# When GpSimd issues its scatters of rows and of weighted outputs in a sparse mixture of experts

## The chip, the cores and the metric

The kernel runs on one core of a Trainium2 chip. The time is device microseconds (us) of that core from a run of the whole program; lower is better. The core has five engines that run side by side and meet at semaphores: TensorE (PE, with its weight loads as PEld), VectorE (DVE), ScalarE (ACT), GpSimd (POOL) and SyncE (SP), which here only issues transfers.

## What is computed

Two layers, each a gated cross attention and a gated mixture of experts, over 8192 tokens of 128 channels. The change lies in the last mixture, which sends each token to the best two of eight experts:

```python
logits = jnp.einsum('bsd,de->bse', x, Wg)
top_vals, top_idx = jax.lax.top_k(logits, TOP_K)          # 2 of 8
probs = jax.nn.softmax(top_vals, axis=-1)
...
    u = jnp.einsum('bsd,dh->bsh', x, W1[e])
    v = jnp.einsum('bsd,dh->bsh', x, W2[e])
    h = u * jax.nn.sigmoid(u) * v
    y = jnp.einsum('bsh,hd->bsd', h, W3[e])
    out = out + y * weights[..., e][..., None]
```

It runs on the layer-normed x, and its result is added to x with a gate.

## The kernel before

**Groups and sends.** The tokens are worked on in 16 groups of 512 (four tiles of 128). The dense part (mixture of layer 0, attention of layer 1, routing for the last mixture) runs over the groups in a software pipeline. Once a group is routed, its rows are *sent*: POOL issues eight indirect transfers a group (two choices times four tiles, line 1208), each of 128 rows of 130 floats, into a table in HBM sorted by expert (`sorted_rows`). Groups 14 and 15 are the last ones and are sent while the sparse part already runs.

**The sparse mixture.** The sorted table is cut into 135 tiles of 128 rows, each of one expert (`DTILES` = 135). The loop over them is written out as *steps*, one function `sparse(t)` an engine. In step t, SP has loaded the rows of tile t (line 1168, seven buffers), PE transposes them (L1977), multiplies tile t-3 with the expert's two first matrices (L1965) and tile t-6 with its last one (L1982), ACT copies weights (L1728) and applies silu (L1734), and DVE keeps the transposed rows (`d_xT`, L1466, one per step and the first thing of a step), multiplies the hidden values (L1471), scales the output of tile t-6 by the token's share (L1484, into one of 32 buffers `shares`) and copies weights (L1490). PE ends a step by adding one to the semaphore `ends_mm`; DVE begins its step t by waiting for that. PE in turn may be a few steps ahead of DVE: its step t needs what DVE kept in step t-3.

**Contributions.** The scaled output of each tile is written to HBM by one indirect transfer of POOL, 128 rows of 128 floats (`keep_share`, line 1224, tile name `contributions`), at the place of each row's token. 135 of them are issued. At the end the contributions are loaded back by group and added to X. For groups 0 to 13 that begins at step 88.

**What sets the order on POOL.** POOL's instructions stand in the order of the code and run in it. During the sparse mixture each of its transfers waits for a step that is written by hand: `scatter_paced(n, steps)` issues the eight sends of group n, the i-th behind the end of step `steps[i]` on PE; `keep_share(t, step)` issues the contribution of tile t behind the end of `step` and behind DVE's share t. Both go through `after_step`, a wait on `ends_mm`. A share can leave at step t+7 at the earliest. In the kernel before, the sends of group 14 are tied to steps 6 to 10, six contributions to steps 11 to 14, the sends of group 15 to steps 15 to 20, and the other contributions follow ten steps behind the earliest step, a distance that shrinks by one every eight tiles and is gone at tile 86.

**Who waits for POOL.** DVE takes a share's buffer again 32 tiles later and waits for the contribution that left it (`kept`, line 1482; first in step 38). SP waits for the sends of groups 14 and 15 before it loads tile 56, and for contributions from step 89 on, before it loads them back.

Of the kernel before, what the change touches and what calls it, by code (L numbers as in the profile page):

```python
# [32 lines left out]
DTILES = 2 * G * GW // P + E1 - 1  # L33
# [32 lines left out]
def wait_alone(eng, semaphore, value):  # L66

    eng.wait_ge(semaphore, value)
    eng.nop(nofuse=True)
# [696 lines left out]
def within(n):  # L766
    return 0 <= n < G
# [215 lines left out]
def mixtures_and_attention(nc, sb, psum, sem, c, a, X, dispatch, out):  # L983
# [71 lines left out]
    HIDDEN, OUT = 3, 6  # L1055
# [62 lines left out]
    def blocks_kept(eng, blocks):  # L1118

        for i in range(8):  # L1120
            tiles = sum(min(4, DTILES - 4 * b) for b in range(i, blocks, 8))
            eng.wait_ge(kept[i], 16 * tiles)
# [9 lines left out]
    def group_sent(eng, n):  # L1132

        eng.wait_ge(dispatch.sent[n % 2], 16 * 2 * GT * (n // 2 + 1))

    with nc.Block() as block:
# [41 lines left out]
        @block.gpsimd  # L1178
        def _(pool):
            def spread_deviation(ln, n):  # L1180
                if within(n):
                    ln.deviation(pool, n)
                    ln.offset(pool, n)

            def deviation1(n):
                if within(n):
                    ln1.deviation(pool, n)

            def number_rows(n):

                if within(n):
                    if n >= 2:
                        group_sent(pool, n - 2)
                    for k in range(2):
                        last = pool.tensor_copy(send[n % 2][k][:, :, D], dispatch.places[:, k, bass.ts(n, GT)])
                    last.then_inc(numbered, 1)

            def scatter(n, which):
                if within(n):
                    if which[0] == 0:  # L1200
                        pool.wait_ge(numbered, n + 1)
                        pool.wait_ge(top1.op_done, top1.ops * (n + 1))
                        wait_alone(pool, place_step, PLACE_STEPS * (n + 1))
                    if which[0] == GT:
                        wait_alone(pool, second_row_ready, n + 1)
                    for i in which:
                        k, j = i // GT, i % GT
                        pool.indirect_dma_start(dispatch.rows, bass.IndirectOffsetOnAxis(ap=slots[n % 2][:, k, j:j + 1], axis=0),  # L1208
                                                send[n % 2][k][:, j, :], None).then_inc(dispatch.sent[n % 2], 16)

            def after_step(step):

                wait_alone(pool, ends_mm, min(step, DTILES + OUT - 1) + 1)

            def scatter_paced(n, steps):
                for i, step in enumerate(steps):
                    after_step(step)
                    scatter(n, (i,))

            def keep_share(t, step):  # L1220

                wait_alone(pool, share_ready, t + 1)
                after_step(step)
                pool.indirect_dma_start(dispatch.contributions, bass.IndirectOffsetOnAxis(ap=token[:, t % KEEP:t % KEEP + 1], axis=0),  # L1224
                                        shares[t % KEEP], None).then_inc(kept[t // 4 % 8], 16)

            pool.memset(w_padded[:].rearrange("p t n -> p (t n)"), 0.0)
            pool.memset(chosen[:].rearrange("p t e -> p (t e)"), 0.0).then_inc(set_up, 1)
            for i in STEPS:
                spread_deviation(ln2, i - 5)  # L1230
                scatter(i - 6, (0, 1))
                deviation1(i - 3)
                scatter(i - 6, (2, 3))
                spread_deviation(ln, i + 1)
                scatter(i - 6, (4,))
                number_rows(i - 5)
                scatter(i - 6, (5, 6, 7))
            spread_deviation(ln2, 14)
            number_rows(14)
            scatter_paced(13, (0, 0, 1, 1, 2, 2, 3, 3))  # L1240
            spread_deviation(ln2, 15)
            number_rows(15)
            scatter_paced(14, (6, 6, 7, 8, 8, 9, 10, 10))
            for t, step in enumerate((11, 12, 12, 13, 14, 14)):
                keep_share(t, step)
            scatter_paced(15, (15, 16, 16, 17, 18, 18, 19, 20))
            for t in range(6, DTILES):
                keep_share(t, t + OUT + 1 + max(0, 10 - (t - 6) // 8))
            blocks_kept(pool, BLOCKS)

        @block.vector
# [875 lines left out]
```

## Time and profile before

| | us |
|---|---|
| median of 3 runs | 858.91 (858.59 to 859.61) |
| the profiled execution | 859.59 |
| its span, first to last instruction | 857.8 |

The rows further down come from the profiled execution. Times in them are from the span's start. A timeline row has start, duration, engine, line, operation, what is written and read, how many instructions, and in brackets the idle time of the engine before it and what ended it ("issue": nothing that the profile shows; "remote": a semaphore whose giver the profile doesn't name). A row of a table of stretches has the stretch, its length, then busy time and number of instructions of an engine, then the granted clock of TensorE (1.00 is full speed, 2.4 GHz), the busy share of the transfer engines, and GB/s. Starts of PE's matmuls are recorded and their ends are modelled. Steps are found by counting the rows of L1466, one for each.

### The profile page before, as it was taken

How to read it: one execution, taken by the hardware profiler on the slowest of the kernel's cores; microseconds unless marked ns; L12 is line 12 of the kernel's file. 1: busy time of each engine (PE TensorE's matmuls, PEld its weight loads, DVE VectorE, ACT ScalarE, POOL GpSimd, SP SyncE). 2: the span in 40 equal slices, each digit the busy share in tenths (PEclk: the TensorE clock that was granted, in tenths of full speed). 3: DMA queues.
4: the chain of work that ended last, by engine and by line, in shares of the span. 5: the costliest groups of instructions: out<-in, count | busy, mean ns of one | idle time of the engine just before them, and what ended most of it. 6: DMA issues, size and time to landing. Idle time of an engine off the chain costs nothing. (4 is left out here: it accounts for less than half of the span.)

```text
span 857.8 us, 27845 instructions
## 1 busy us (share of the span) xinstructions
PE 752.8 (88%) x9217; PEld 588.2 (69%) x9217; DVE 675.5 (79%) x2969; ACT 552.7 (64%) x1195; POOL 462.9 (54%) x498
## 2 busy tenths in 40 slices
PE   4899999999998979989989988777689898999991
PEld 2567666666666646766766765567689788888991
DVE  3899999999998968887888887646567666578993
ACT  2778787788787656888888786535445444444550
POOL 3455445544565011366776776664556666565564
PEclk9999999999999979999999999977899999999996
DMA  9101100010000010011111111121233333266764
GB/s 255 57 25 34 34 21 21 21 43 21 21 21 3 2 41 1 21 35 43 51 48 43 51 45 38 47 68 47 54 73 94 89 81 81 76 180 201 228 186 128
DMA packets 59177, 56.41 MB, mean 66 GB/s; under 512 B 9976, under 2 KB 49177, under 8 KB 59081
## 3 DMA queue, kind: packets, MB, share of 16 engines
q1 hardware_dynamic: 41736, 33.16, 14.6%
q0 software_dynamic: 8416, 17.38, 6.1%
q10 hardware_dynamic: 8928, 4.70, 1.9%
q8 instruction: 47, 0.77, 0.4%
q14 instruction: 50, 0.40, 0.2%
HBM read 32.65 MB, written 22.56 MB: 64 GB/s over the span
## 5 line engine op out<-in xcount | busy, mean ns | idle before, releaser
L1224 POOL DMA_INDIRECT contributions<-v_heads,d_token x135 | 133.2, 986 | 87.3 <-PE bc_bank L1982 47.8
L1208 POOL DMA_INDIRECT sorted_rows<-r_send,r_slots x128 | 127.0, 992 | 47.0 <-issue 40.6
L1965 PE MATMUL bc_bank<-d_xT,d_w 128*128 128x128 f32 x608 | 88.1, 291 | 13.4 <-DVE v_heads L1484 6.6
L1466 DVE COPY d_xT<-bc_bank 128x128 f32<-128x128 f32 x135 | 38.4, 284 | 73.5 <-PE bc_bank L1982 48.1
L512 POOL TENSOR_SCALAR a_k_heads<-a_kT,first 128x512 f32<-128x512 f32 x60 | 93.4, 1569 | 3.7 <-ACT a_kT L567 3.7
L1965 PEld LDWEIGHTS bc_bank<-d_xT,d_w 128*128 128x128 f32 x608 | 79.3, 204 | 16.8 <-DVE d_xT L1466 15.3
L1728 ACT COPY d_w<-w 128x512 f32 x135 | 83.4, 618 | 1.8 <-issue 0.6
L429 DVE TENSOR_REDUCE a_neg_max<-a_scores 128x16 f32<-128x1024 f32 x64 | 78.0, 1219 | 7.0 <-PE a_scores L680 6.1
L705 PE MATMUL a_probsT_bank<-first,a_probs 128*128 128x128 f32 x512 | 80.2, 279 | 0.3
L426 DVE TENSOR_REDUCE a_denom<-a_probs 128x16 f32<-128x1024 f32 x64 | 78.4, 1224 | 1.7 <-issue 1.3
L598 ACT COPY a_probsT<-a_probsT_bank 128x512 f32<-128x512 f32 x128 | 74.7, 584 | 6.3 <-PE a_probsT_bank L705 6.3
L591 ACT ACTIVATE a_probs<-a_scores 128x1024 f32<-128x1024 f32 x64 | 65.6, 1025 | 19.2 <-PE a_scores L691 19.2
L1734 ACT ACTIVATE b_weighted<-bc_pair 128x256 f32<-128x256 f32 x59 | 22.8, 387 | 79.4 <-PE bc_bank L1965 48.7
L680 PE MATMUL a_scores<-a_k_heads,a_qT 32*64 32x256 f32 x1024 | 70.8, 391 | 2.5 <-ACT a_kT L567 2.3
L1965 PE MATMUL bc_pair<-d_xT,d_w 128*128 128x128 f32 x472 | 65.6, 283 | 6.0 <-DVE d_xT L1466 4.1
L74 POOL TENSOR_SCALAR a_rstd<-a_stats 128x4 f32<-128x4 f32 x16 | 3.7, 233 | 121.1 <-DVE a_stats L396 121.1
L705 PEld LDWEIGHTS a_probsT_bank<-first,a_probs 128*128 128x128 f32 x512 | 57.9, 142 | 15.2 <-issue 12.5
L1965 PEld LDWEIGHTS bc_pair<-d_xT,d_w 128*128 128x128 f32 x472 | 59.2, 197 | 8.4 <-DVE d_xT L1466 5.8
L1804 PE MATMUL bc_bank<-b_xnT,w 128*128 128x512 f32 x96 | 51.1, 645 | 13.0 <-ACT c_kT L1653 7.1
L1734 ACT ACTIVATE b_hidden<-bc_bank 128x256 f32<-128x256 f32 x68 | 26.4, 390 | 43.4 <-PE bc_pair L1965 20.8
L1982 PE MATMUL bc_bank<-w_in,b_hidden 128*128 128x128 f32 x272 | 44.2, 280 | 4.6 <-issue 3.1
L1855 PE MATMUL bc_bank<-w,b_weighted 128*128 128x128 f32 x384 | 46.8, 278 | 0.1
(236 smaller groups left out, 2022.7 us busy)
## 6 DMA issues: line engine op xcount, KB each, us to landing
d_rows<-sorted_rows SPq DMA_DIRECT2D x135, 65.0 KB
X<-in_x SPq DMA_DIRECT2D x16, 256.0 KB, 3.1
b_hidden<-contributions SPq DMA_DIRECT2D x8, 512.0 KB
b_weighted<-contributions SPq DMA_DIRECT2D x8, 512.0 KB
out_x<-X ACTq DMA_DIRECT2D x16, 256.0 KB
ctxT<-in_ctx_T SPq DMA_DIRECT2D x16, 192.0 KB, 3.0
c_ctxT<-in_ctx_T SPq DMA_DIRECT2D x16, 192.0 KB
contributions<-v_heads,d_token POOLq DMA_INDIRECT x135
```

The source lines that it names most:

```text
L426: dve.reduce_sum(denom[:], probs[u % 2][:].rearrange("p (h k) -> p h k", k=S), AX_X).then_inc(sum_done, 1)
L429: dve.tensor_reduce(neg_max[:], scores[u % 2][:].rearrange("p a (h k) -> p (a h) k", k=S), AX_X, ALU.max, negate=True).then_inc(max_done, 1)
L512: last = pool.tensor_scalar(keys_of_head(par, j), kT[:], c.head_of_group[:, j:j + 1], None, ALU.mult)
L591: act.activation(probs[(u + 1) % 2][:], scores[(u + 1) % 2][:].rearrange("p a n -> p (a n)"), ACT.Exp, scale=SCALE0).then_inc(exp_done, 1)
L598: act.copy(probsT[u % 2][:, half * HU // 2:(half + 1) * HU // 2, :].rearrange("p u q -> p (u q)"), probsT_bank[:]).then_inc(pT_ev, 1)
L680: last = pe.matmul(scores[u % 2][S * b:S * b + S, s, bass.ts(h, 4 * S)], qT[par][rows_in, h, tile, :], k_heads[par][rows_in, tile, h].rear ...
L705: last = pe.transpose(probsT_bank[:, bass.ts(k, P)], probs[u % 2][:, bass.ts(half * HU // 2 + k, P)], c.ident[:])
L1208: pool.indirect_dma_start(dispatch.rows, bass.IndirectOffsetOnAxis(ap=slots[n % 2][:, k, j:j + 1], axis=0), send[n % 2][k][:, j, :], None) ...
L1224: pool.indirect_dma_start(dispatch.contributions, bass.IndirectOffsetOnAxis(ap=token[:, t % KEEP:t % KEEP + 1], axis=0), shares[t % KEEP], ...
L1728: act.copy(w12[t % W12][:], c.w12[:, bass.ds(experts[t % 4], 1)].rearrange("d a i h -> d (a i h)")).then_inc(w12_ready, 1)
L1804: pe.matmul(h_bank[k][:], c.w1_0[:, 2 * k:2 * k + 2, :].rearrange("d e h -> d (e h)"), xnT[n % 2][:], start=True, stop=True).then_inc(h_mm ...
L1965: last = pe.matmul(uv(m)[:, bass.ts(i, P)], w12[m % W12][:, bass.ts(i, P)], xT[m % TURNED][:], start=True, stop=True)
```

## The change

Only the table of steps on POOL changes:

```diff
             scatter_paced(13, (0, 0, 1, 1, 2, 2, 3, 3))
             spread_deviation(ln2, 15)
             number_rows(15)
-            scatter_paced(14, (6, 6, 7, 8, 8, 9, 10, 10))
-            for t, step in enumerate((11, 12, 12, 13, 14, 14)):
-                keep_share(t, step)
-            scatter_paced(15, (15, 16, 16, 17, 18, 18, 19, 20))
-            for t in range(6, DTILES):
-                keep_share(t, t + OUT + 1 + max(0, 10 - (t - 6) // 8))
+            scatter_paced(14, (14, 14, 15, 15, 16, 16, 17, 17))
+            scatter_paced(15, (18, 18, 19, 19, 20, 20, 21, 21))
+            for t in range(DTILES):
+                keep_share(t, max(t + OUT + 1, 22 + 10 * t // 13))
             blocks_kept(pool, BLOCKS)
```

`OUT` is 6. All 16 sends now stand behind steps 14 to 21, two a step. The contributions come behind them: the first at step 22, then 13 in ten steps, until the rule t+7 takes over at tile 61. Number, size and content of the transfers are the same.

On POOL, from the last four sends of group 14 to the first contributions (names: `r_send` the rows of a group by choice, `v_heads` the memory in which the shares lie, `d_ends_mm` the end of a step on PE, `d_share` DVE's share), as one piece of the difference:

```order
 L1208 DMA sorted_rows<-r_send_1,r_slots 67456x130 [waits d_ends_mm,r_second_row]
 L1208 DMA sorted_rows<-r_send_1,r_slots 67456x130 [waits d_ends_mm] x3
-L1224 DMA contributions<-v_heads,d_token 18304x128 [waits d_share,d_ends_mm] x6
 L1208 DMA sorted_rows<-r_send_0,r_slots 67456x130 [waits d_ends_mm,r_place_step,r_numbered,r_op_done]
 L1208 DMA sorted_rows<-r_send_0,r_slots 67456x130 [waits d_ends_mm] x3
 L1208 DMA sorted_rows<-r_send_1,r_slots 67456x130 [waits d_ends_mm,r_second_row]
 L1208 DMA sorted_rows<-r_send_1,r_slots 67456x130 [waits d_ends_mm] x3
-L1224 DMA contributions<-v_heads,d_token 18304x128 [waits d_share,d_ends_mm] x129
+L1224 DMA contributions<-v_heads,d_token 18304x128 [waits d_share,d_ends_mm] x135
```

Six contributions moved from between the two groups of sends to behind both; the steps for which the rows wait are in the diff.

On DVE, step 38, the first that waits for a contribution to have left its buffer, before:

```order
L1466 COPY d_xT<-bc_bank 128x128 [waits d_ends_mm]
L1467 COPY d_ends<-d_rows 128x2
L1471 TENSOR_TENSOR b_weighted<-b_weighted,bc_pair 128x256 [waits d_silu_done]
L1483 CAST d_token<-d_ends 128x4 [waits d_row_read,d_kept0]
L1484 TENSOR_SCALAR v_heads<-bc_bank,d_ends 128x128
L1490 ISA
L1490 COPY w_in<-w 128x256
```

and now:

```order
L1464 COPY d_xT<-bc_bank 128x128 [waits d_ends_mm]
L1465 COPY d_ends<-d_rows 128x2
L1469 TENSOR_TENSOR b_weighted<-b_weighted,bc_pair 128x256 [waits d_silu_done]
L1481 CAST d_token<-d_ends 128x4 [waits d_row_read,d_kept0]
L1482 TENSOR_SCALAR v_heads<-bc_bank,d_ends 128x128
L1488 ISA
L1488 COPY w_in<-w 128x256
```

Nothing moved here but the line numbers; only when `d_kept0` comes can differ.

## Rows read from the trace of the kernel before

**Rows 1.** The page's first part: busy time, share, instructions.

```profile
PE 752.8 (88%) x9217; PEld 588.2 (69%) x9217; DVE 675.5 (79%) x2969; ACT 552.7 (64%) x1195; POOL 462.9 (54%) x498
```

**Rows 2.** Stretches of the sparse mixture, L1466 alone: its count is the steps.

```profile
602.00:624.00 22.00, 2.31 (x8) 0.77 0.23 62
624.00:640.40 16.40, 2.29 (x8) 1.00 0.27 65
640.40:652.80 12.40, 2.25 (x8) 1.00 0.37 93
652.80:727.10 74.30, 11.60 (x41) 0.97 0.33 84
727.10:768.10 41.00, 6.26 (x22) 0.97 0.43 121
768.10:837.20 69.10, 11.78 (x42) 1.00 0.71 204
```

**Rows 3.** The first two stretches, sends (L1208) alone.

```profile
602.00:624.00 22.00, 7.84 (x8) 0.77 0.23 62
624.00:640.40 16.40, 7.74 (x8) 1.00 0.27 65
```

**Rows 4.** The same two, contributions (L1224) alone.

```profile
602.00:624.00 22.00, 3.83 (x4) 0.77 0.23 62
624.00:640.40 16.40, 1.92 (x2) 1.00 0.27 65
```

**Rows 5.** The later stretches, columns PE, PEld, DVE, ACT, POOL; POOL issues contributions only.

```profile
640.40:652.80 12.40, 12.40 (x112) 12.14 (x112) 10.24 (x50) 6.36 (x15) 6.80 (x7) 1.00 0.37 93
652.80:727.10 74.30, 65.79 (x531) 62.43 (x530) 46.79 (x218) 35.28 (x86) 45.41 (x47) 0.97 0.33 84
727.10:768.10 41.00, 36.98 (x300) 35.11 (x298) 26.72 (x122) 17.07 (x42) 24.86 (x26) 0.97 0.43 121
768.10:837.20 69.10, 64.83 (x535) 61.30 (x535) 61.77 (x263) 35.43 (x83) 42.14 (x42) 1.00 0.71 204
```

**Rows 6.** Timeline of POOL in steps 9 to 11.

```profile
607.15 1.01 POOL L1208 DMA_INDIRECT sorted_rows<-r_send,r_slots  x1 [2.20 <-PE bc_bank L1982]
...
614.80 0.96 POOL L1208 DMA_INDIRECT sorted_rows<-r_send,r_slots  x1 [0.30 <-issue]
617.87 0.96 POOL L1224 DMA_INDIRECT contributions<-v_heads,d_token  x1 [2.11 <-remote]
```

**Rows 7.** Timeline of PE: ends of steps 11 and 12, begin of step 13.

```profile
610.67 0.61 PE L1982 MATMUL bc_bank<-w_in,b_hidden 128*128 128x128 f32 x4
...
613.01 0.61 PE L1982 MATMUL bc_bank<-w_in,b_weighted 128*128 128x128 f32 x4
618.19 2.04 PE L1965 MATMUL bc_bank<-d_xT,d_w 128*128 128x128 f32 x8 [4.56 <-DVE v_heads L1484]
```

**Rows 8.** Timeline of DVE: begins of steps 11, 12 and 14.

```profile
617.13 0.29 DVE L1466 COPY d_xT<-bc_bank 128x128 f32<-128x128 f32 x1 [5.08 <-remote]
...
619.83 0.28 DVE L1466 COPY d_xT<-bc_bank 128x128 f32<-128x128 f32 x1
...
624.06 0.29 DVE L1466 COPY d_xT<-bc_bank 128x128 f32<-128x128 f32 x1 [1.42 <-PE bc_bank L1982]
```

**Rows 9.** Timeline of POOL, steps 37 to 45: bursts of five and of four contributions.

```profile
661.61 0.96 POOL L1224 DMA_INDIRECT contributions<-v_heads,d_token  x1 [1.34 <-PE bc_bank L1982]
...
666.78 0.96 POOL L1224 DMA_INDIRECT contributions<-v_heads,d_token  x1 [0.30 <-issue]
669.49 0.96 POOL L1224 DMA_INDIRECT contributions<-v_heads,d_token  x1 [1.75 <-PE bc_bank L1982]
...
676.02 0.96 POOL L1224 DMA_INDIRECT contributions<-v_heads,d_token  x1 [1.66 <-PE bc_bank L1982]
```

**Rows 10.** Timeline of PE: end of step 38.

```profile
663.91 0.61 PE L1982 MATMUL bc_bank<-w_in,b_hidden 128*128 128x128 f32 x4
```

**Rows 11.** Timeline of DVE: begin of step 38.

```profile
668.76 0.29 DVE L1466 COPY d_xT<-bc_bank 128x128 f32<-128x128 f32 x1 [3.22 <-remote]
```

## The prediction

> **What bounds the kernel now.** I read the page's first part, then the sparse mixture by stretches of steps, then single bursts in the timelines. The page makes PE the busiest engine at 88% of the span, and POOL one of the emptiest at 54% [rows 1]. By that alone a change that only shifts POOL's transfers would seem free. The stretches say otherwise. In steps 22 to 29 the eight steps take 12.40 us, PE is busy for all 12.40 of them, and POOL issues only 7 transfers: 1.55 us a step. In steps 30 to 70, 41 steps take 74.30 us, 1.81 each, with 47 transfers, and PE is busy for only 65.79 of it [rows 2, 5]. Per step the work of PE, DVE and ACT is the same there, and what differs most is how many transfers POOL issues for each step. So: what do the engines wait for?
>
> The timelines show it. In steps 37 to 45 POOL works in bursts. Five contributions begin at 661.61 and the next burst at 669.49, 7.88 us later; that one has four and lasts 6.53 us until the next at 676.02. Four steps pass in each. Within a burst the transfers stand 1.26 us apart (0.96 and 0.30 of issue) [rows 9]. PE's step 38 is over by its row at 663.91 + 0.61 = 664.52. DVE, which waits for nothing else there, begins step 38 at 668.76, after 3.22 us idle, 1.02 us behind the end of POOL's last transfer of the burst (666.78 + 0.96 = 667.74) [rows 9 to 11]. The same at step 11, in the burst of sends: PE's step 11 is over at 610.67 + 0.61 = 611.28, POOL's seven sends from 607.15 on end at 614.80 + 0.96 = 615.76, and DVE begins step 11 at 617.13, 1.37 us later and after 5.08 us idle [rows 6 to 8]. **My reading:** while POOL issues indirect transfers back to back, PE's signal that a step is over reaches DVE, ACT and POOL itself only about 1 us after the burst. PE may be three steps ahead, then it waits for DVE, and one cycle of four steps lasts as long as POOL's burst.
>
> **A price for this.** The two cycles differ by one transfer and by 7.88 - 6.53 = 1.35 us. I take 1.37 us a transfer and 0.255 us a step (four transfers and four steps: 5.48 + 1.02 = 6.50, measured 6.53; five: 7.87, measured 7.88). The long stretches test it. 47 transfers and 41 steps give 64.4 + 10.5 = 74.9 (measured 74.30); 26 and 22 give 41.2 (41.00); 42 and 42 give 68.3 (69.10); 8 + 2 and 8 give 15.7 (16.40); 7 and 8 give 11.6 (12.40) [rows 2 to 5]. Only steps 6 to 13 cost clearly more, 22.0 us against 12 x 1.37 + 2.0 = 18.5, since the last groups' routing is woven into them.
>
> **The change part by part.**
>
> *Steps 6 to 13 lose all twelve of their transfers (8 sends, 4 contributions) [rows 3, 4].* DVE then begins step 11 where PE ends it, at 611.3 and not at 617.13. The routing of group 15, which stands behind step 11 on DVE, waits for small matmuls that PE does between steps 11 and 12, and keeps its length: step 12 follows step 11 by 2.70 us now [rows 8], so 614.0. PE's step 13 need not wait until 618.19; it follows step 12's end at 613.62 [rows 7] by 1.55 us, as the steps 22 to 29 with a fully busy PE do (the clock should stay up, since it fell in this stretch, to 0.77 on average, behind idle times of PE [rows 2, 7]), and step 14 by 1.55 more, so DVE begins step 14 near 616.7 and not at 624.06 [rows 8]: **-7.3 us**. At the least it is the delay of step 11 alone, 5.8. At the most the eight steps would take 1.55 each, 12.4 for 22.0: -9.6.
>
> *Steps 14 to 21 have 16 sends for 8 sends and 2 contributions [rows 3, 4].* 16 x 1.37 + 8 x 0.255 = 24.0 for 16.4: **+7.6**.
>
> *Steps 22 to 29 have 11 contributions for 7* (tiles 0 to 10 by the table): 17.1 for 12.4, **+4.7**. *Steps 30 to 70 have 53 for 47*: 72.6 + 10.5 = 83.1 for 74.3, **+8.8**. *Steps 71 to 92 have 22 for 26*, as the contributions have caught up: 30.1 + 5.6 = 35.8 for 41.0, **-5.2**. From step 93 on both tables are the same, and so is the end: **0**.
>
> Sum: -7.3 + 7.6 + 4.7 + 8.8 - 5.2 = **+8.6 us**. In short: twelve transfers leave steps that would be bound by other things without them, and enter steps that POOL's count sets (102 for 90 between steps 14 and 92). They cost 12 x 1.37 = 16.4 there and gave 7.3 where they were. The profiled execution took 859.59, so 868.2 on it; it lies 0.7 above the median of 858.91, which gives **867.5 us**.
>
> *Waits.* None is added. The earliest buffer that DVE takes again is in step 38, and its contribution is issued behind step 22 to 24. SP wants the sends of both groups before tile 56, which it loads some six steps ahead; they are out soon after step 21. Nothing else on POOL stands behind the moved rows: the layer norm of group 15 and the numbering of its rows come ahead of them in both. The cost of these is nothing, covered by 14 steps or more. If POOL fell ten steps behind its table, the buffers would begin to bind; then they would only say the same as the price above.
>
> *Bounds.* A transfer costs at least its distance of 1.26 us in a burst, if it costs anything, and at most what the stretch of steps 71 to 92 has per transfer, 41.0 / 26 = 1.58. With the gain's ends: 12 x 1.26 - 9.6 = +5.5 and 12 x 1.58 - 5.8 = +13.2.
>
> *A rule against this.* PE's end is modelled, so the trace shows when DVE was released but not when PE was done. The Trainium skill says so too (Perfetto Trace Analysis, the summary of the profiler window per engine type: the end of a TensorE instruction is estimated, and the way of the semaphore isn't shown). It also states that PE and ACT never wait on anyone, and that DVE and GpSimd alone lock each other out of a port (SBUF — State Buffer, Who interferes with whom). By that rule POOL's bursts couldn't hold PE's steps back, and the sum would be nothing. The rows speak against it, since release follows the burst's end twice by 1.0 and 1.4 us and a cycle grows by 1.35 us with one more transfer.
>
> **The rivals.**
>
> *Cover (faster).* The hold is real, but POOL idles 1.3 to 1.8 us between bursts [rows 9] and is busy for only 45.41 of 74.30 us in steps 30 to 70 [rows 5]. Twelve more transfers are 15.1 us of issue; from step 14 to 92 (144.1 us) the 90 of before take 113.4, so 30.7 us are open. If they go into these gaps, only the early gain is left: 858.9 - 7.3 = **851.6 us**. It decides if a fifth transfer no longer lengthens a cycle. Against it: it does, by 1.35 us.
>
> *No link (same).* Bursts and waits only keep step, because POOL waits for the same signal. Then the cycle length has another cause, nothing is won at step 11 either, and the time stays at **858.9**, within 1 us.
>
> *Dearer bursts (slower still).* With eight sends in a cycle PE idles for about six of its 12 us. After an idle time of 4.56 us PE's eight matmuls of L1965 took 2.04 us, where four of L1982 had taken 0.61 before it [rows 7], and the clock was 0.77 on average in that stretch. PE's four steps of a cycle, 6.2 us at full speed, take 12.4 at half. If half of the difference stands behind the bursts and not under them, two cycles in steps 14 to 21 cost 3.1 us more each, and the later ones a little: about **875 us**.
>
> **How the numbers follow.** The forecast has 0.64, dearer bursts 0.13, cover 0.15, no link 0.08. So slower by over 0.2% (1.7 us, about what a measurement of this kernel can tell from no change) 0.77, within it 0.08, faster 0.15. The range takes in the bounds (864.4 to 872.1) and reaches toward the others: 857.5 to 874.5 leaves out the cover case and the tail of the dear one.
>
> **What would show each step.** In the profile of the changed kernel: no transfer of POOL between the eight sends of group 13 and step 14; DVE's step 11 within 1 us of PE's; DVE's step 14 near 617; step 22 at 616.7 + 24.0, so near 641, about where it is now (640.4); steps 30 to 70 in cycles with five and six contributions, 2.0 us a step; the lead of before at step 93 is 8 to 9 us and stays. I am wrong if cycles of six transfers last no longer than those of five, if step 14 comes no earlier, or if DVE waits at L1483 for its buffers.

## The result, and the profile after

| | before | after |
|---|---|---|
| median, us | 858.97 (858.59 to 859.61) | 870.08 (867.82 to 872.85) |
| ratio, 95% interval | | 1.0107 (1.0076 to 1.0138) |
| profiled execution, us | 859.59 | 867.82 |
| its span, us | 857.8 | 866.0 |

The changed kernel is slower by 9.2 us (6.5 to 11.9) by the ratio of the table, by 11.1 between the two medians, and by 8.2 between the two profiled executions. The forecast was +8.6 and 867.5 us, the range 857.5 to 874.5. I read the same stretches of steps as before, cut at the rows of the copy that begins a step (L1466 before is L1464 now; two lines went above it). Columns: the stretch, its length, DVE's busy time in that copy and its count, the granted clock, the share and the rate of the transfers.

```profile
601.37:614.67 13.30, 2.31 (x8) 1.00 0.18 39
614.67:638.79 24.12, 2.32 (x8) 0.86 0.24 61
638.79:657.42 18.63, 2.27 (x8) 0.82 0.29 73
657.42:740.31 82.89, 11.65 (x41) 0.95 0.32 82
740.31:777.02 36.71, 6.27 (x22) 0.98 0.45 127
777.02:845.88 68.86, 11.62 (x41) 1.00 0.71 205
```

Beside [rows 2] these are steps 6 to 13, 14 to 21, 22 to 29, 30 to 70, 71 to 92 and 93 to 133. Step 6 begins 0.7 us earlier than before (601.37 for 602.07; nothing moved ahead of it, so I count it as scatter). Then: -8.7, +7.7, +6.2, +8.6, -4.3, -0.05, together 9.5. With the 0.7 at the start that is +8.8 at step 134, of which 0.6 is given back behind it. The sends, line 1208, in the same windows: none in the first, 15 in the second, and one slips into the third. The columns are those of the table above, with POOL's busy time in the sends and their count.

```profile
601.37:614.67 13.30, 0.00 (x0) 1.00 0.18 39
614.67:638.79 24.12, 13.96 (x15) 0.86 0.24 61
```

Step 11, where DVE waited 5.08 us before [rows 8], now follows PE. DVE's timeline (start, duration, in brackets the idle time before and what ended it):

```profile
607.77 0.29 DVE L1464 COPY d_xT<-bc_bank 128x128 f32<-128x128 f32 x1 [0.50 <-PE bc_bank L1980]
...
609.22 0.29 DVE L1464 COPY d_xT<-bc_bank 128x128 f32<-128x128 f32 x1 [0.23 <-PE bc_bank L1980]
...
611.91 0.28 DVE L1464 COPY d_xT<-bc_bank 128x128 f32<-128x128 f32 x1
...
613.01 0.29 DVE L1464 COPY d_xT<-bc_bank 128x128 f32<-128x128 f32 x1
...
614.68 0.29 DVE L1464 COPY d_xT<-bc_bank 128x128 f32<-128x128 f32 x1 [0.37 <-PE bc_bank L1980]
```

And the bursts of contributions are longer. POOL's timeline, the burst that answers to [rows 9]: six transfers, and the next one begins 698.02 - 688.69 = 9.33 us after the first.

```profile
688.69 0.95 POOL L1224 DMA_INDIRECT contributions<-v_heads,d_token  x1 [1.90 <-PE bc_bank L1980]
689.95 0.96 POOL L1224 DMA_INDIRECT contributions<-v_heads,d_token  x1 [0.30 <-issue]
...
695.05 0.96 POOL L1224 DMA_INDIRECT contributions<-v_heads,d_token  x1 [0.30 <-issue]
698.02 0.96 POOL L1224 DMA_INDIRECT contributions<-v_heads,d_token  x1 [2.02 <-remote]
```

So the picture of the prediction is there. Whether it is also the cause, and whether the sum came out for the right reasons, is what the experiments are for.

### The profile page after: what moved, and what is told of

Read it like the earlier page. It is cut to its first block and busy times, and to the rows that moved or that the text cites. A ratio compares the mean times of both kernels' runs of the same rounds, so it can differ in the third digit from the quotient of the medians.

```text
span 866.0 us, 27845 instructions
## 1 busy us (share of the span) xinstructions
PE 752.6 (87%) x9217; PEld 588.4 (68%) x9217; DVE 676.1 (78%) x2969; ACT 551.9 (64%) x1195; POOL 460.0 (53%) x498
## 5 line engine op out<-in xcount | busy, mean ns | idle before, releaser
L1224 POOL DMA_INDIRECT contributions<-v_heads,d_token x135 | 131.3, 973 | 85.4 <-PE bc_bank L1980 43.3
L1208 POOL DMA_INDIRECT sorted_rows<-r_send,r_slots x128 | 126.4, 988 | 59.8 <-issue 41.9
L1963 PE MATMUL bc_bank<-d_xT,d_w 128*128 128x128 f32 x608 | 89.3, 293 | 17.2 <-DVE d_xT L1464 12.6
L1464 DVE COPY d_xT<-bc_bank 128x128 f32<-128x128 f32 x135 | 38.4, 285 | 82.4 <-PE bc_bank L1980 40.6
L705 PEld LDWEIGHTS a_probsT_bank<-first,a_probs 128*128 128x128 f32 x512 | 57.6, 141 | 15.2 <-issue 12.4
```

The source lines that it names most:

```text
L705: last = pe.transpose(probsT_bank[:, bass.ts(k, P)], probs[u % 2][:, bass.ts(half * HU // 2 + k, P)], c.ident[:])
L1963: last = pe.matmul(uv(m)[:, bass.ts(i, P)], w12[m % W12][:, bass.ts(i, P)], xT[m % TURNED][:], start=True, stop=True)
```

## The experiments

They ran in four series, each on one chip together with the kernel before. The kernel before took 865.8 us in the first series, 866.1 in the second, 800.4 in the third and 799.2 in the fourth. The first two behave like the chip of the timed pair (859.0), the last two don't, and that turned out to be a result of its own. *Hold* is short for the prediction's reading: while POOL issues indirect transfers back to back, PE's signal that a step is over comes late.

### Twelve more transfers

The number of transfers is raised and nothing is moved. Behind every fourth contribution POOL sends rows of group 15 again, into a table that nobody reads.

```diff
+    EXTRA = [15, 19, 23, 27, 31, 35, 39, 43, 47, 51, 55, 59]
...
                 keep_share(t, t + OUT + 1 + max(0, 10 - (t - 6) // 8))
+                if t in EXTRA:
+                    i = EXTRA.index(t)
+                    pool.indirect_dma_start(dispatch.spare, bass.IndirectOffsetOnAxis(ap=slots[1][:, i // GT % 2, i % GT:i % GT + 1], axis=0),
+                                            send[1][i // GT % 2][:, i % GT, :], None).then_inc(dispatch.sent[1], 16)
...
```

> The kernel before with twelve extra indirect transfers of 128 rows, one behind every fourth contribution from tile 15 to tile 59, so in steps 31 to 70; they write rows of group 15 once more into a spare table that nobody reads. Hold (POOL's transfers keep PE's signal back, 1.37 us a transfer): 12 x 1.37 = +16.4 us over the kernel before, all of it in steps 30 to 70 (74.3 becomes about 90), DVE and PE idle longer there. Cover (POOL's gaps of 1.3 to 1.8 us between bursts take them): +0 to +3. No link (bursts and waits only keep step): +0, within 1 us.

Measured: 884.66 us for 865.81, ratio 1.0214 (1.0176 to 1.0252), so +18.5 us (15.2 to 21.8). The stretches of steps 30 to 70, 71 to 92 and 93 to 133 of this kernel:

```profile
653.11:744.62 91.51, 11.75 (x42) 0.89 0.30 79
744.62:786.84 42.22, 6.26 (x22) 0.96 0.42 115
786.84:857.85 71.01, 11.80 (x42) 1.00 0.70 199
```

91.51 us where 74.30 stood on the chip of the timed pair: +17.2 for twelve transfers, 1.43 each. *Cover* and *no link* fall. POOL's gaps between bursts don't take a transfer, since they are part of the hold: a burst of six lasts from 670.26 to the next at 679.65, 9.39 us.

### The same with half the rows

```diff
-                    pool.indirect_dma_start(dispatch.spare, bass.IndirectOffsetOnAxis(ap=slots[1][:, i // GT % 2, i % GT:i % GT + 1], axis=0),
-                                            send[1][i // GT % 2][:, i % GT, :], None).then_inc(dispatch.sent[1], 16)
+                    pool.indirect_dma_start(dispatch.spare, bass.IndirectOffsetOnAxis(ap=slots[1][0:P // 2, i // GT % 2, i % GT:i % GT + 1], axis=0),
+                                            send[1][i // GT % 2][0:P // 2, i % GT, :], None).then_inc(dispatch.sent[1], 16)
```

> As the kernel with twelve extra transfers, but each of them has 64 rows in place of 128. Hold by time on POOL: the price goes with how long POOL issues. If a transfer of 64 rows takes as long on POOL as one of 128, +16.4 us again; if it takes half as long, about +8. A rival within the theory, that the rows' data on their way are what holds the signals: +8 whatever POOL's time is. Cover and no link: +0 to +3.

Measured: 884.92 us, ratio 1.0210 (1.0176 to 1.0243), the same as with whole transfers. POOL's group of these transfers (busy time, mean ns of one) shows that half the rows save it next to nothing:

```profile
L1226 POOL DMA_INDIRECT contributions<-v_heads,d_token x135 | 132.4, 981 | 92.5 <-PE bc_bank L1989 47.0 <-issue 34.0 <-remote 6.6
...
L1253 POOL DMA_INDIRECT spare_rows<-r_send,r_slots x12 | 10.9, 911 | 3.7 <-issue 3.4 <-DVE v_heads L1491 0.3
```

The price goes with the number of transfers (0.91 us of issue each, and 0.97 for the same twelve with 128 rows) and not with their bytes, which were halved. The rival that the data on their way do the holding falls.

### The contributions without POOL

SP writes the contributions with plain transfers, tile after tile; the placement by token is left out.

```diff
+            def keep_plain(eng, t):
+                eng.wait_ge(share_ready, t + 1)
+                eng.dma_start(dispatch.contributions[bass.ts(t, P), :], shares[t % KEEP]).then_inc(kept[t // 4 % 8], 16)
...
                     sp.dma_start(rows[n % ROWS][:], dispatch.rows[bass.ds(firsts[n - t], P), :]).then_inc(d_loaded[n % ROWS], 16)
+                    if n >= 13:
+                        keep_plain(sp, n - 13)
...
-                pool.indirect_dma_start(dispatch.contributions, bass.IndirectOffsetOnAxis(ap=token[:, t % KEEP:t % KEEP + 1], axis=0),
-                                        shares[t % KEEP], None).then_inc(kept[t // 4 % 8], 16)
```

> The kernel before with POOL's 135 contributions taken out. The same data are written by SP with plain transfers, in the order of the tiles; the placement by token is left out, so the sums at the end take other rows. POOL then issues only the sends in the sparse part. Hold: steps 22 to 134 run at what PE's own work needs, 1.5 us a step or a little more, so steps 30 to 70 take 60 to 64 us for 74.3, steps 71 to 92 32 to 35 for 41.0, and from step 93 on 64 to 67 for 68.9; with 3 to 5 us in steps 6 to 21 the kernel takes 825 to 834 us. No link: 859, within 2 us. Cover: the same as no link.

Measured: 822.08 us for 865.81, ratio 0.948 (0.944 to 0.952), even more than expected. Steps 30 to 70 and 71 to 92, with the busy times of PE, PEld, DVE, ACT and POOL:

```profile
652.41:711.82 59.41, 59.41 (x535) 59.41 (x534) 48.15 (x218) 37.54 (x83) 0.00 (x0) 1.00 0.42 102
711.82:743.84 32.02, 32.02 (x290) 32.02 (x288) 27.21 (x122) 20.45 (x45) 0.00 (x0) 1.00 0.49 136
```

59.41 us for 41 steps is 1.45 each, and PE never stops. In the kernel before the same steps take 1.81. Some 15 us of the 44 hang on this stretch alone.

### POOL busy with something else

SP writes as above, and behind the same waits POOL computes in place of each transfer, about as long as one.

```diff
-                pool.indirect_dma_start(dispatch.contributions, bass.IndirectOffsetOnAxis(ap=token[:, t % KEEP:t % KEEP + 1], axis=0),
-                                        shares[t % KEEP], None).then_inc(kept[t // 4 % 8], 16)
...
+                pool.tensor_tensor(busy[1][:], busy[0][:], c.minus_half[:], ALU.pow).then_inc(numbered, 1)
+                wait_alone(pool, numbered, G + 2 * t + 1)
+                pool.tensor_copy(busy[2][:], busy[1][:]).then_inc(numbered, 1)
```

> As the kernel with the contributions on SP, but POOL works in their place: behind the same waits it does one power and one copy of 128x4, about 1.2 us on POOL together, which is a transfer's distance in a burst. The placement by token is left out here too. If it is the indirect transfer that holds PE's signals: as without POOL's contributions, 825 to 836 us. If any work of POOL of that length does it (a port, or the order of waits on POOL): near 859. No link: 859.

Measured: 843.62 us, ratio 0.973 (0.969 to 0.977). That is neither number, so I looked where the 21.5 us over the kernel without POOL lie. Steps 30 to 70 take exactly as long as there, though POOL is busy for 47.94 us of them and works in every step; below them, DVE's and ACT's waits in that stretch (us in total, times, longest):

```profile
653.62:713.03 59.41, 59.41 (x535) 59.41 (x534) 48.18 (x218) 37.53 (x83) 47.94 (x79) 1.00 0.43 104
```

```profile
ACT b_weighted L1746 <- PE bc_pair L1977: 11.2, 20, 0.6
DVE d_xT L1478 <- PE bc_bank L1994: 11.0, 39, 0.3
```

No wait of DVE is longer than 0.3 us. The 21.5 us come behind the last step, which begins 1.3 us later than without POOL's work: a power and a copy follow each other every 1.47 us, POOL is behind with them, and the kernel ends when it has done the rest (the last copy starts at 840.59, of a span of 842.4). The mean of the total would have hidden that. So it isn't enough that POOL is busy all the time; PE's signals come late only with the indirect transfers.

### POOL issues, but plainly

```diff
-                pool.indirect_dma_start(dispatch.contributions, bass.IndirectOffsetOnAxis(ap=token[:, t % KEEP:t % KEEP + 1], axis=0),
-                                        shares[t % KEEP], None).then_inc(kept[t // 4 % 8], 16)
+                pool.dma_start(dispatch.contributions[bass.ts(t, P), :], shares[t % KEEP]).then_inc(kept[t // 4 % 8], 16)
```

> The kernel before, with the contributions still issued by POOL behind the same waits, but as plain transfers in the order of the tiles; the placement by token is left out. If the hold comes with an address per row (the indirect form): steps 30 to 70 at about 1.45 us each as with the contributions on SP, and 822 to 830 us on the chip of the first kernels. If any transfer that POOL issues does it: 1.8 us a step, near the kernel before.

Measured: 824.45 us for 866.13, ratio 0.952 (0.949 to 0.954), and steps 30 to 70 take 59.41 us again. So a transfer a step issued by POOL doesn't hold by itself. A plain transfer takes POOL 0.54 us (73.2 us for 135), and that leaves one point open: in this stretch they stand about 1.45 us apart, with some 0.9 us idle between them, and form no bursts like the indirect ones. Whether plain transfers back to back would hold PE's signals wasn't run.

### The change in halves

First the contributions by the changed rule, with the sends as before:

```diff
             scatter_paced(14, (6, 6, 7, 8, 8, 9, 10, 10))
-            for t, step in enumerate((11, 12, 12, 13, 14, 14)):
-                keep_share(t, step)
             scatter_paced(15, (15, 16, 16, 17, 18, 18, 19, 20))
-            for t in range(6, DTILES):
-                keep_share(t, t + OUT + 1 + max(0, 10 - (t - 6) // 8))
+            for t in range(DTILES):
+                keep_share(t, max(t + OUT + 1, 22 + 10 * t // 13))
```

> One half of the change: the sends of groups 14 and 15 as before, the contributions by the changed rule (first at step 22). By the count of transfers (hold): steps 6 to 13 lose four of twelve, worth 1.5 us at the least (what steps 11 to 13 took less in the changed kernel, 5.46 for 6.92) and 5.5 at the most; steps 14 to 21 have 8 for 10, 13.0 us for 16.4; the steps from 22 on as in the changed kernel, +4.7 +8.8 -5.2; together between +0.9 and +3.4 us over the kernel before. If it is the late catching up of the contributions that costs, whatever the count: +8 to +11 us. If the sends are what costs: 0 or less.

Then the sends as changed, with the contributions by the table of before as far as it lies at step 22 or later:

```diff
+            scatter_paced(14, (14, 14, 15, 15, 16, 16, 17, 17))
+            scatter_paced(15, (18, 18, 19, 19, 20, 20, 21, 21))
+            for t in range(DTILES):
+                keep_share(t, max(22, t + OUT + 1 + max(0, 10 - (t - 6) // 8)))
```

> The other half: the sends of groups 14 and 15 behind steps 14 to 21 as in the change, the contributions by the table of before, but none ahead of step 22; so 13 of them fall in steps 22 to 29 and 47 in 30 to 70 as before. By the count (102 transfers in steps 14 to 92, as in the changed kernel): the same as the changed kernel, +7 to +11 us, with the loss in steps 14 to 29 (24 and 20 us for 16.4 and 12.4) and none in 30 to 92. If the contributions' late catching up is the cost: 0 to +2.

And the changed kernel beside them:

> The changed kernel once more, beside its halves on one chip: +7 to +11 us.

| | us | ratio | over before |
|---|---|---|---|
| before | 866.13 | | |
| contributions moved | 875.67 | 1.0114 (1.0097 to 1.0130) | +9.9 |
| sends moved, contributions from 22 on | 876.53 | 1.0114 (1.0098 to 1.0130) | +9.9 |
| changed kernel | 875.53 | 1.0111 (1.0091 to 1.0132) | +9.6 |

The last column is worked out from the ratio.

The second met what it was expected to, in its stretches too: steps 14 to 21 took 24.34 us, 22 to 29 21.52, 30 to 70 75.56. The first didn't: +0.9 to +3.4 was expected and +9.9 measured. The first three stretches, first with the contributions moved:

```profile
604.70:625.71 21.01, 2.29 (x8) 0.87 0.20 52
625.71:642.82 17.11, 2.32 (x8) 0.96 0.25 59
642.82:658.76 15.94, 2.25 (x9) 0.97 0.30 77
```

and then of the changed kernel in the same series:

```profile
605.99:619.29 13.30, 2.30 (x9) 1.00 0.17 39
619.29:643.55 24.26, 2.32 (x8) 0.86 0.24 60
643.55:662.31 18.76, 2.27 (x9) 0.82 0.29 72
```

Between these two only sends move: eight leave steps 6 to 13 and give 7.7 us, steps 14 to 21 take 7.2 more and steps 22 to 29, with one late send and a lower clock, 2.8. In these two profiles that is about 2 us for the sends; by the medians of the table it is nothing (875.67 and 875.53). Either way it is the small part. (The sends alone moved, with the six contributions left at steps 11 to 14, wasn't run.) What all three kernels share is that the six contributions of steps 11 to 14 go behind step 22. Where they were, they cost little: steps 6 to 21 take 21.01 + 17.11 = 38.1 us without them and took 22.00 + 16.40 = 38.4 with them [rows 2]. (The latter is from the chip of the timed pair, since the kernel before has no profile from this one. The medians of the two differ by 0.8%, some 0.3 us here.) The two kernels with extra transfers have the order of before in these steps, and took 38.7 and 39.4 us. So the six cost 0.3 to 1.3 us together, and runs of one order differ by as much.

The timelines say why. In the kernel before, three of them are issued from 617.87 [rows 6] to 621.36. No signal of PE is due in that time: PE begins step 13 only at 618.19 [rows 7] and does it at a granted clock of 0.50, until 621.30, and DVE follows at once.

```profile
620.40 0.96 POOL L1224 DMA_INDIRECT contributions<-v_heads,d_token  x1 [0.30 <-issue]
```

```profile
620.24 1.06 PE L1982 MATMUL bc_bank<-w_in,b_weighted 128*128 128x128 f32 x4
```

```profile
621.34 0.29 DVE L1466 COPY d_xT<-bc_bank 128x128 f32<-128x128 f32 x1 [0.37 <-PE bc_bank L1982]
```

In the kernel with the contributions moved, POOL has nothing to do in that place. Its first eight sends end at 618.3, and it idles until the table lets it go on behind step 15. On DVE, step 11 and the routing behind it:

```profile
628.97 1.09 POOL L1208 DMA_INDIRECT sorted_rows<-r_send,r_slots  x1 [10.65 <-PE bc_bank L1980]
```

```profile
615.54 0.29 DVE L1464 COPY d_xT<-bc_bank 128x128 f32<-128x128 f32 x1 [3.24 <-PE bc_bank L1980]
...
619.89 0.39 DVE L806 MAX8 r_sorted<-bc_bank 128x8 f32<-128x8 f32 x4 [3.19 <-remote]
```

Steps 12 to 14 then go at the pace of the routing and of a PE at half clock. Six contributions need 6 x 1.26 = 7.6 us on POOL, and find room in the 10.65 us in which it would wait anyway. The first row of DVE shows another thing: a signal of PE may also get through within a burst. It is 3.0 us late (PE's step 11 is over at 612.50), but comes between the sends that begin at 614.8 and 616.1.

### More and less lead for PE

If a cycle is one burst and as many steps as PE may do on its own, the lead sets how many steps share the 1 to 1.5 us that a cycle costs beside its transfers. Less lead:

```diff
     def step_before(t):
-        return t - 2 if t < FIRST else t - 4
+        return t - 2
```

> The kernel before with PE allowed less lead: from step 20 on it waits for what DVE kept two steps earlier, not three or four. Without a hold PE needs no such lead (a step of it takes 1.45 us and DVE's 1.06), and the time stays within 2 us. Hold: a cycle of POOL's burst takes 1.26 us for each transfer and about 1.46 us once, and holds as many steps as PE may do on its own. Three steps a cycle for four: steps 30 to 70 take 47 x 1.26 + 41/3 x 1.46 = 79 us for 74.3, steps 71 to 92 43.5 for 41.0, from 93 on 73 for 68.9: +11 us in all. Two steps a cycle: +25. If the 0.255 us a step of the prediction's price is a cost of the step and not of the cycle: 0.

More lead:

```diff
-    HIDDEN, OUT = 3, 6
+    HIDDEN, OUT = 4, 8
...
-                keep_share(t, t + OUT + 1 + max(0, 10 - (t - 6) // 8))
+                keep_share(t, t + 7 + max(OUT - 6, 10 - (t - 6) // 8))
```

> The kernel before with PE allowed more lead: the hidden values of a tile are multiplied four steps behind its transposition, not three, and the output eight steps behind, not six, so that PE may run four steps ahead of DVE. The table of steps on POOL stays, except that the last contributions come two steps later. Hold: five steps a cycle for four: steps 30 to 70 take 47 x 1.26 + 41/5 x 1.46 = 71 us for 74.3, steps 71 to 92 39 for 41.0, from 93 on 65 for 68.9, with 2 to 3 us for two more steps at the end: -4 to -7 us. No link or a cost of each step: +2 to +3 us, the two steps alone.

and, so as to have the stretches of before beside them:

> The kernel before as it is, for its profile on the chip of this series: the two halves of the change and the changed kernel ran on a chip where the kernel before took 866 us and not 859, and their stretches need stretches of before from such a chip. The same transfers in each stretch; where the 7 us more lie is open.

Measured: before 800.42 us (796.99 to 805.54, 23 runs), less lead 799.24 with ratio 0.9997 (0.9966 to 1.0027), more lead 802.12 with 1.0015 (0.9990 to 1.0039). None of it tests the question, since this chip shows no hold at all. The kernel before, unchanged, from steps 30 to 70 on:

```profile
626.10:685.51 59.41, 59.41 (x535) 59.41 (x534) 49.08 (x218) 37.58 (x83) 45.35 (x47) 1.00 0.40 107
685.51:717.53 32.02, 32.02 (x289) 32.02 (x288) 27.75 (x121) 20.47 (x45) 24.40 (x25) 1.00 0.51 148
```

It has POOL's 47 indirect transfers in the stretch and its 45.35 us of issue, as in [rows 2, 5], and takes 59.41 us, to the hundredth what the kernels without them took on the first two chips. POOL goes on without a pause, and DVE begins each step 0.3 us behind PE, in the middle of it:

```profile
659.43 0.29 DVE L1466 COPY d_xT<-bc_bank 128x128 f32<-128x128 f32 x1 [0.29 <-PE bc_bank L1982]
...
660.88 0.29 DVE L1466 COPY d_xT<-bc_bank 128x128 f32<-128x128 f32 x1 [0.30 <-PE bc_bank L1982]
```

```profile
660.08 0.96 POOL L1224 DMA_INDIRECT contributions<-v_heads,d_token  x1 [0.31 <-issue]
661.34 0.96 POOL L1224 DMA_INDIRECT contributions<-v_heads,d_token  x1 [0.30 <-issue]
```

The kernel with more lead ran once more, and met a chip of that kind again:

> The kernel with PE allowed four steps of lead, once more, since the first series of it ran where no hold is seen. Where the kernel before takes 859 to 866 us: five steps a cycle, steps 30 to 70 at about 71 us for 74 to 76, from step 93 on 65 for 69 to 71, -4 to -7 us in all; if each step has its cost whatever the lead, +2 to +3. Where the kernel before takes near 800: +1 to +2 again, for the two more steps at the end.

Measured: 801.64 us for 799.17, ratio 1.0042 (1.0019 to 1.0065): two more steps at the end, and nothing won. Whether more lead pays where PE's signals are held is still open; it is the first thing that I would run next.

## Why the prediction came out, point by point

The forecast was 867.5 us and 870.08 were measured, slower as said and within the range. The hold and its price where transfers are the limit were right. The account of what the transfers cost where they stood before was not, and that the total came out in spite of it was luck in part.

**The bound.** Right, and now shown for the chips on which it holds. Twelve more transfers cost 18.5 us, 135 fewer gave 43.7, and POOL's other work and its plain transfers cost the steps nothing. A rule that the prediction weighed, from the Trainium skill (SBUF — State Buffer, Who interferes with whom), has PE wait for nobody. It is said there of the ports of SBUF, and the runs neither bear it out nor break it in its own words: PE goes on with its next steps during a burst, as the recorded starts of its matmuls show, and what it has finished is seen late. Read as "POOL's bursts can't cost PE anything" it would have given no change, and that is wrong by 9 us here.

**The price.** 1.37 us a transfer and 0.255 a step holds where POOL's table is always behind. In the extra-transfer kernel 59 transfers in steps 30 to 70 would be 91.3 us, and 91.51 were measured; a cycle of six would be 9.24 and was 9.33. In the changed kernel, steps 30 to 70 were forecast at 83.1 and took 82.89, steps 71 to 92 at 35.8 and took 36.71. In the second series the latter took 39.09, because POOL was further behind and issued 24 transfers there and not 22; for 24 the price gives 38.5.

**Steps 6 to 13.** Forecast -7.3, measured -8.7, within the bounds. DVE began step 14 at 614.68, not at 616.7. I had kept PE's times of before up to step 11 (611.3; it was 609.22). Of the 2.1 us between them 0.7 is that step 6 began earlier, and 1.3 that step 8 did. The moved transfers gave neither. Step 8 was late in the profile of before because PE did it at a granted clock of about half: its eight matmuls of L1965 took 1.89 us there and take 1.13 now, after the same 2.02 us of idle time. With the first send in its place, but PE at full clock, step 8 follows step 7 by 1.70 us in the kernel with the contributions moved, as it does in the changed kernel (1.71) and not by 2.98. Without this 1.3 us the gain is 7.4, beside 7.7 between the two kernels of the second series.

**Steps 14 to 21.** Forecast +7.6, measured +7.7, with 15 sends inside and not 16: by the price that is 22.6 us, and 24.12 were measured. One send fell into steps 22 to 29, with 12 transfers for 11: 18.5 by the price, 18.63 measured, and so +6.2 for +4.7. The granted clock was 0.86 and 0.82 in the two stretches, from 1.00 before. That is where the rival of dearer bursts had its place, and by the 1.5 us of steps 14 to 21 it got a part of what it wanted.

**Where the reasons were wrong.** The prediction said in short that twelve transfers cost 12 x 1.37 where they go and gave 7.3 where they were. The step that failed is to count all twelve alike in steps 6 to 13, and to take 16.40 us in steps 14 to 21 as the cost of 8 + 2 transfers. POOL waits there for its table and for the routing, so the stretch isn't set by the count. With 8 sends and no contribution steps 14 to 21 took 16.79 us in the kernel with the contributions on SP and 17.11 in the one with the contributions moved (3.3 of them before the first send), not 13.0, and with two contributions more 16.40. In steps 6 to 13 the eight sends gave 7.7 us (21.01 to 13.30), and the four contributions 1.0 at the most (22.0 to 21.01). The sends' half of the change is between nothing (medians) and 2 us (stretches). Most of the loss, if not all, is that of six contributions, taken out of a place where they cost 0.3 to 1.3 us together and put where each costs 1.37 or more: 8.2 us by the price, and 9.9 (8.4 to 11.3) measured with the contributions alone. My sum hit the total because in the full change the wrong term for steps 14 to 21 (8 + 2 transfers, 16.4 measured) was taken from the trace of before, and the new count there was high enough for the price to hold. For the half it missed by 6.5 us or more.

**Waits.** None at the buffers: the line that waits for them (L1481 now) has no idle time before it in the whole trace. The loss of 8.86 us at step 93 was 8.81 at step 134, so nothing comes back while the tables are the same.

## What to carry to other kernels

Price an edit by the marginal cost of the place, not of the operation: in a stretch that is set by something else the same transfers were nearly free, and moving them behind the others cost 1.4 us each or more. Test a sum by its halves, since two wrong terms can give the right total, as here. And before tuning an order to a hold between engines, look whether the other chips that the kernel will run on show it: on two of those that these runs met there is no hold for such a change to work on. What this change costs there was not run.

## What the runs showed of the hardware

- On the chips of the timed pair and of the first two series, while POOL issues indirect transfers back to back, what PE has finished is mostly seen by DVE and ACT only 1.0 to 1.6 us after the burst's end (DVE 668.76 and ACT 668.70 behind 667.74, DVE 619.89 behind 618.33), and in the rows shown POOL's own next burst begins 1.3 to 2.1 us after it. Now and then a signal gets through within the burst. PE's ends are modelled, so the traces don't tell whether the signal is late or the last of the matmul's work. In steps that wait for this it costs 1.4 us a transfer, whether it has 128 rows or 64. POOL's vector work back to back doesn't do it, nor do its plain transfers at one a step.
- On two other chips the same program shows nothing of it. The kernel before takes 859 to 866 us on the former and 799 to 800 on the latter. Both kinds agree up to the first indirect transfer (370.8 and 371.3 us into the span; the second window below begins at 371.20). From there to the first step of the sparse part they need 213.0 and 198.4 us, and from there to the end 274.0 and 229.1:

```profile
370.80:583.79 212.99, 185.79 (x1369) 138.91 (x1367) 164.88 (x1073) 157.36 (x313) 149.56 (x188) 0.97 0.16 47
583.79:857.80 274.01, 228.20 (x1803) 216.96 (x1803) 184.54 (x844) 122.69 (x287) 158.33 (x165) 0.92 0.43 119
```

```profile
371.20:569.68 198.48, 180.62 (x1369) 138.03 (x1367) 167.08 (x1073) 157.62 (x313) 148.60 (x188) 0.97 0.17 51
569.68:798.80 229.12, 207.79 (x1803) 206.56 (x1803) 186.86 (x844) 132.19 (x287) 161.86 (x165) 0.94 0.51 142
```

  The first pair is the kernel before on the chip of the timed runs, the second the same kernel in the third series; the transfers' share and rate are higher in the latter because the same work takes less time. What differs between the chips, or whether it is a state that a chip can leave, the runs don't tell. The changed kernel didn't run where there is no hold.
